# Splitting h into two fp16 parts in a serial recurrence on VectorE: a scan and a rounding constant, and the gates summed one after another

## The reference

```
def step(carry, xs):
    h, c = carry
    xi_t, xf_t, xg_t, xo_t = xs
    i_t = sigmoid(xi_t + h @ V_i)
    f_t = sigmoid(xf_t + h @ V_f)
    g_t = tanh(xg_t + h @ V_c)
    o_t = sigmoid(xo_t + h @ V_o)
    c_new = h * c + i_t * g_t
    h_new = o_t * tanh(c_new)
    return ((h_new, c_new), h_new)
(_, _), hs = lax.scan(step, (h0, c0), (xi, xf, xg, xo))
```

## Time and profile before

| | us |
|---|---|
| median of 3 runs | 3307.72 |
| lowest and highest | 3303.53, 3311.19 |
| span of the profiled execution | 3296.9 |
| VectorE busy | 1953.7 (59%) |
| TensorE busy, matmuls | 1510.9 (46%) |
| ScalarE busy | 1441.9 (44%) |
| GpSimd busy | 169.9 (5%) |

### The profile page before, as it was taken

How to read it: one execution, slowest core, us unless ns; L and a number is a source line. 1 busy time by engine, 2 the same in 40 slices (tenths; PEclk the granted TensorE clock), 3 DMA queues, 4 the chain that set the end, 5 groups by cost and what they waited for, 6 DMA issues and landing times.

```text
span 3296.9 us, 86333 instructions
## 1 busy us (share of the span) xinstructions
PE 1510.9 (46%) x26414; PEld 1141.6 (35%) x26414; DVE 1953.7 (59%) x13086; ACT 1441.9 (44%) x8446; POOL 169.9 (5%) x130
## 2 busy tenths in 40 slices
PE   4989575434343434333443434343434343434343
PEld 4444323333333333333333333333333333333333
DVE  5557896555555555555555555555555555555555
ACT  5331134444444444444444444444444444444444
POOL 0620271000000000000000000000000000000000
PEclk8999885555555555555555555555555555555555
DMA  6010000000000000000000000000000000000000
GB/s 225 1 32 0 0 5 1 2 3 2 3 2 3 2 3 2 3 2 3 2 2 3 2 3 2 3 2 3 2 3 2 3 2 3 2 2 2 3 2 15
DMA packets 13012, 29.04 MB, mean 9 GB/s; under 512 B 1971, under 2 KB 9654, under 8 KB 10422
## 3 DMA queue, kind: packets, MB, share of 16 engines
q1 hardware_dynamic: 10406, 22.02, 1.9%
q10 hardware_dynamic: 2064, 0.55, 0.1%
HBM read 21.52 MB, written 1.05 MB: 7 GB/s over the span
## 4 chain that ended last, share of the span: by engine, by line
ACT 37%; PE 37%; DVE 15%; issue 9%; DMA 1%; SPq 0%; DVEq 0%; POOL 0%; ACTq 0%; POOLq 0%
PE psum L490 21%; ACT work L663 18%; ACT work L659 11%; DVE work L984 11%; ACT work L655 8%; PE psum L412 4%; PE psum L494 3%; PE psum L353 2%; PE psum L474 2%; PE psum L473 2%; PE psum L364 1%; DVE work L898 1%; DVE FT L935 1%; DMA work<-in_adj_dram 1%; PE psum L392 0%
## 5 line engine op out<-in xcount | busy, mean ns | idle before, releaser
L490 PE MATMUL psum<-work,MASK 128*128 128x1 f16 x18432 | 951.5, 168 | 1656.3 <-DVE work L984 1582.5
L490 PEld LDWEIGHTS psum<-work,MASK 128*128 128x128 bf16 x18432 | 802.7, 107 | 1817.5 <-DVE work L984 1741.0
L655 ACT ACTIVATE work<-psum 128x1 f32<-128x1 f32 x2048 | 351.2, 172 | 1471.0 <-PE psum L494 1471.0
L979 DVE TENSOR_SCALAR work<-work 128x1 f32<-128x1 f32 x2048 | 314.6, 154 | 732.1 <-ACT work L659 732.1
L663 ACT ACTIVATE work<-psum,work 128x1 f32<-128x1 f32 x2048 | 720.2, 352 | 0.0
L494 PE MATMUL psum<-work,MASK 128*128 128x1 f16 x6144 | 575.5, 168 | 0.0
L984 DVE CUSTOM_DVE_ANT_0 work<-work 128x1 f16<-128x1 f32 x2048 | 331.5, 162 | 295.3
L494 PEld LDWEIGHTS psum<-work,MASK 128*128 128x128 f16 x6144 | 432.3, 107 | 0.0
L990 DVE SCALAR_TENSOR_TENSOR work<-psum,work 128x1 f32<-128x1 f32 x2048 | 430.7, 210 | 0.0
L659 ACT ACTIVATE work<-psum 128x1 f32<-128x1 f32 x2048 | 414.9, 203 | 20.8 <-PE psum L494 20.8
L987 DVE TENSOR_TENSOR work<-work 128x1 f16<-128x1 f32 x2048 | 332.3, 162 | 72.1
(11 more groups left out here) (132 smaller groups left out, 1005.2 us busy)
## 6 DMA issues: line engine op xcount, KB each, us to landing
work<-in_adj_dram SPq DMA_DIRECT2D x16, 1024.0 KB, 5.3
work<-in_L_ffn_Wd_dram SPq DMA_DIRECT2D x4, 512.0 KB, 6.0
out_dram<-work SPq DMA_DIRECT2D x4, 256.0 KB, 2.4
work<-in_L_ffn_bd_dram SPq DMA_DIRECT2D x1, 512.0 KB, 6.8
W<-in_L_ffn_W_dram ACTq DMA_DIRECT2D x1, 256.0 KB, 2.8
watt<-in_L_gnn_w_att_dram ACTq DMA_DIRECT2D x2, 64.0 KB, 7.2
work<-in_L_gnn_Wq_dram SPq DMA_DIRECT2D x1, 64.0 KB, 8.1
Wfc<-in_L_gnn_W_fc_dram ACTq DMA_DIRECT2D x1, 64.0 KB, 5.8
```

What stands on the lines that cost most here:

```text
L490: nc.tensor.matmul(bank(NGATE * k + gate)[:, col:col + 1], Vparts[:, gate, part, :], h1[:, q:q + 1], start=False, stop=False, skip_group_c ...
L655: nc.scalar.activation(sig_i[:, q], bank(NGATE * k)[:, col:col + 1], ACT.Sigmoid).then_inc(i_ready, 1)
L979: v.tensor_scalar(o_scaled[:, q], sig_o[:, q], SCALE_H, None, ALU.mult).then_inc(o_scaled_ready, 1)
```

## The change

h = (2^8 o) * tanh_c is split in another way. The constant ROUND_H = 1.5 * 2^20 is added to a number below 2^8 in fp32 and taken away again; what is left is the number rounded to a multiple of 1/8, which fp16 holds exactly.

- Line 979's instruction now writes two numbers, -2^8 o and 2^8 o, around a constant 0: `o_signs` times sig_o, sig_o being a scalar operand per partition.
- h1: a scan over three elements that starts from tanh_c. It multiplies by 2^8 o and adds 0, multiplies by 1 and adds ROUND_H, multiplies by 1 and adds -ROUND_H. Its third element, in fp16, is h1.
- h2: one instruction over three elements, (-2^8 o, 0, 2^8 o) * tanh_c + (-ROUND_H, ROUND_H, 0), whose sum over the elements goes out as h2 (accum_out, which adds a readout of the accumulator). It reads nothing that the scan wrote, and there is no wait between the two.
- The fp32 product into `ring_h` is an instruction of its own, and hc waits for it (h_ready).
- The waits ahead of the scan stand in the order o_scaled_ready, tanh_ready; those ahead of hc in the order h_ready, c_ready.
- TensorE: upper i (three), the wait for h2, lower i, upper g (three), lower g, upper o (three), lower o.
- Ten small constants are set ahead of the loop.

```
@@ tensor
                     pe.wait_ge(h1_ready, t + 1)
                     upper(0, 2, 1, 0)
-                    upper(1, 2, 1, 0)
-                    upper(2, 2)
                     pe.wait_ge(h2_part_ready, t + 1)
                     lower(0, i_summed)
+                    upper(1, 2, 1, 0)
                     lower(1, g_summed)
-                    upper(2, 1, 0)
+                    upper(2, 2, 1, 0)
                     lower(2, o_summed)
...
@@ vector
                     dve.wait_ge(o_ready, t + 1)
-                    v.tensor_scalar(o_scaled[:, q], sig_o[:, q], SCALE_H, None, ALU.mult).then_inc(o_scaled_ready, 1)
-
+                    v.tensor_scalar(o_signed[:, u % 2, 0:3:2], o_signs, sig_o[:, q], None, ALU.mult).then_inc(o_scaled_ready, 1)
+
+                    dve.wait_ge(o_scaled_ready, t + 1)
                     dve.wait_ge(tanh_ready, t + 1)
-                    dve.wait_ge(o_scaled_ready, t + 1)
-
-                    v.tensor_tensor_reduce(h1[:, r], tanh_c[:, q], o_scaled[:, q], 1.0, 0.0, ALU.mult, ALU.add,
-                                           ring_h[:, u:u + 1]).then_inc(h1_ready, 1)
-                    dve.wait_ge(h1_ready, t + 2)
-                    v.tensor_tensor(h2[:, r], ring_h[:, u:u + 1], h1[:, r], ALU.subtract).then_inc(h2_part_ready, 1)
+
+                    v.tensor_tensor_scan(h_steps[:, 1 - u % 2, 0:3], o_signed[:, u % 2, 2:5], round_up, tanh_c[:, q],
+                                         ALU.mult, ALU.add).then_inc(h1_ready, 1)
+
+                    v.scalar_tensor_tensor(h_sums, o_signed[:, u % 2, 0:3], tanh_c[:, q], round_back,
+                                           ALU.mult, ALU.add, accum_out=h2[:, r]).then_inc(h2_part_ready, 1)
+                    v.tensor_tensor(ring_h[:, u:u + 1], o_signed[:, u % 2, 2:3], tanh_c[:, q], ALU.mult).then_inc(h_ready, 1)
 
                     dve.wait_ge(hc_ready, t + 1)
                     v.scalar_tensor_tensor(c_[:, q], bank(6 + u % 2)[:, 0:1], sig_i[:, q], hc[:, q],
                                            ALU.mult, ALU.add).then_inc(c_ready, 1)
+                    dve.wait_ge(h_ready, t + 1)
                     dve.wait_ge(c_ready, t + 1)
                     v.scalar_tensor_tensor(hc[:, r], ring_h[:, u:u + 1], 1.0 / SCALE_H, c_[:, q],
                                            ALU.mult, ALU.mult).then_inc(hc_ready, 1)
```

More of the change, by code:

```diff
@@ L28 @@
 SCALE_H = 2.0 ** 8
+ROUND_H = 1.5 * 2.0 ** 20
 FP16_MAX = 65504.0
@@ L144, in build_program @@
         ring_h = region(N + HALF, STEPS)
-        c_, hc, tanh_c, sig_i, sig_o, o_scaled = (region(SMALL + 2 * k, 2) for k in range(6))
-        h1 = region(SMALL + 14, 1).bitcast(FP16)
+        c_, hc, tanh_c, sig_i, sig_o = (region(SMALL + 2 * k, 2) for k in range(5))
         h2 = region(SMALL + 16, 1).bitcast(FP16)
+        o_signed = region(SMALL + 18, 10, "p (q s) -> p q s", q=2)
+        h_steps = region(SMALL + 28, 4).bitcast(FP16).rearrange("p (q s) -> p q s", q=2)
+        h_sums = region(SMALL + 32, 3)
+        round_up = region(SMALL + 36, 3)
+        round_back = region(SMALL + 40, 3)
+        o_signs = region(SMALL + 44, 2)
         result = region(3 * N, N, "p (c t d) -> p c t d", c=NCH, t=TPC)
@@ L198, in build_program @@
         o_scaled_ready, h1_ready, h2_part_ready = sem("o_scaled_ready"), sem("h1_ready"), sem("h2_part_ready")
+        h_ready = sem("h_ready")
         c_ready, hc_ready, hh_ready = sem("c_ready"), sem("hc_ready"), sem("hh_ready")
@@ L489, in upper @@
                         for part in parts:
-                            nc.tensor.matmul(bank(NGATE * k + gate)[:, col:col + 1], Vparts[:, gate, part, :], h1[:, q:q + 1],
+                            nc.tensor.matmul(bank(NGATE * k + gate)[:, col:col + 1], Vparts[:, gate, part, :], h_steps[:, q, 2:3],
                                              start=False, stop=False, skip_group_check=True)
@@ L971, in _ @@
             v.memset(hc[:, 0:1], 0.0).then_inc(hc_ready, 1)
-            v.memset(h1[:, 0:1], 0.0).then_inc(h1_ready, 1)
+            for part, value in ((o_signs[:, 0:1], -SCALE_H), (o_signs[:, 1:2], SCALE_H),
+                                (o_signed[:, :, 1:2], 0.0), (o_signed[:, :, 3:5], 1.0),
+                                (round_up[:, 0:1], 0.0), (round_up[:, 1:2], ROUND_H), (round_up[:, 2:3], -ROUND_H),
+                                (round_back[:, 0:1], -ROUND_H), (round_back[:, 1:2], ROUND_H), (round_back[:, 2:3], 0.0)):
+                chain.step(v.memset(part, value))
+            v.memset(h_steps[:, 0, 2:3], 0.0).then_inc(h1_ready, 1)
             v.memset(h2[:, 0:1], 0.0).then_inc(h2_part_ready, 1)
```

## The result

| | before | after |
|---|---|---|
| median of 4 runs, us | 3305.72 | 3482.49 |
| lowest to highest, us | 3303.53 to 3311.19 | 3477.89 to 3483.36 |
| span of the profiled execution, us | 3296.9 | 3481.6 |

The ratio is 1.0532, 95% interval 1.0517 to 1.0547: the change makes the kernel slower by 177 us. 3538 was forecast, in a range of 3385 to 3650. The spans differ by more, 185 us: after's lies 1.8 under the time of its own run (3483.36), before's lies 6.6 under the lowest of its timed runs.

A forecast was written before the change was run, and what follows sets the result against it. The bound was taken to be the recurrence's 2048 serial steps, 1.35 us each. 0 + 0.04 + 0.07 = 0.11 us a step gives 225 us, plus 5 is +230: span 3527, time 3538 us, range 3385 to 3650.

The forecast's parts named there:

- The h split: Scan and h2 instruction on VectorE: independence buys back what scalar operands cost, 0 us a step (bounds -0.11, +0.08).
- The overlap of 0.08: VectorE: with no wait between, the h2 instruction starts 0.08 us before the scan ends.
- The gates in turn: TensorE's matmul order: lower g runs later, moving tanh of g and tanh of c by +0.04 us a step.
- The order of two waits: Ahead of the scan: tanh_c's wait, now second, is an instruction of its own, +0.07 us a step (bounds 0, 0.08).
- Side paths: hc and the o product beside the chain: both stay hidden, 0 us; hc's late end would cost 0.07.
- rival 1: hc ends last and holds tanh of c: +0.05 us more a step, 3640 us; chance 0.12.
- The small terms: Gate-input steps keep the same sum; longer VectorE program +4 us, ten constants +1 us: +5 us.
- the 10.8: Program start and end outside the profiled span: 10.8 us added to the forecast span of 3527 us.

The follow-up runs named there:

- a_dependent: Changed kernel with one wait added, so that the h2 instruction waits for the scan's h1_ready: 3746.79 us, ratio 1.1325.
- a_free_scan: As a_split_o, with ScalarE writing tanh_c into the scan's input, so the scan has four elements and no scalar operand: 3252.78 us, ratio 0.9825.
- a_oldgates: Changed kernel with the old order of matmuls (seven upper ones before the wait for h2): 3522.84 us, ratio 1.0645.
- a_split_o: Changed kernel with tanh_ready first ahead of the scan and the o product split into two products with constants: 3366.67 us, ratio 1.0177.
- a_waits: Changed kernel with the two waits ahead of the scan back in the old order, tanh_ready first: 3481.76 us, ratio 1.0521.
- b_turn: Kernel before with only the gates' matmuls reordered to sum i, g and o in turn: 3424.06 us, ratio 1.0348.
- b_noscale: Kernel before without line 979; line 984 multiplies by 2^8 itself and waits for tanh_ready, then o_ready: 3300.23 us, ratio 0.9970.
- b_noscale_turn: Kernel before without line 979, line 984 scaling itself, and with the gates summed in turn: 3352.58 us, ratio 1.0126.
- b_waits: Kernel before with only the two waits ahead of line 984 swapped, o_scaled_ready first, tanh_ready second: 3512.88 us, ratio 1.0615.

## Why the prediction was right, and where it was not

**The h split, 0: right.** h2's readout ends at the same time as line 987 did, to 0.01 us, for the reason given: an independence worth 0.13 (a_dependent) is spent on scalar operands. That the scan pays for its own was an inference from other instructions; a_free_scan shows it, at 0.06 us rather than 0.05. For the h2 instruction no run takes the scalar away; its 214 ns against the 159 of line 1007, of the same kind with a constant, stay a comparison. The overlap of 0.08 held too, to 0.01 (0.23 against a start at 0.14).

**The gates in turn, +0.04: a little too much.** Tanh of g moved by 0.04, but now that it doesn't follow close behind the i sigmoid it takes 0.156 us instead of 0.166 (line 657 against line 663 of the pages), so tanh of c moved by 0.03. The prediction called this what the reordering costs. That was right as a sum and wrong as a cause: a_oldgates has the new split with the old order, and there tanh of c starts 0.05 later than before the change (0.97 behind the scan for 0.92). So the split alone would cost that 0.05, by its later first matmul, and the new order takes 0.02 of it back.

**The order of two waits, +0.07: the price right, the order only half the cause.** 0.10 for 0.03 in the profile, and a_split_o takes it away. As a statement about the order alone it was wrong: a_waits shows that the o product came so late that the old order would have cost the same. That the term came out as forecast was in this part luck: the late o product, with its two elements and its scalar operand, would have brought it in either order. The forecast had that product 0.04 ahead of being needed; it ends at 2034.87 and the scan starts at 2034.97, so with a direct wait of 0.03 it was covered by 0.07, but only by the other wait's own price.

**Side paths.** hc ended at 0.83, at the early end of 0.82 to 0.94, 0.11 ahead of tanh of c, so rival 1 did not come. The 0.09 that was taken for ScalarE's second wait is shown by no run; at that price the cover would be nearly gone. The reading of the kernel before was wrong at one place: "line 979 ends at 1.15, 0.15 before it is needed" was no slack. A second wait stood in between, and b_turn, b_noscale and b_noscale_turn show that it held line 984 just as much as tanh of c did. The forecast for the change wasn't hurt, because the scan replaces line 984 and pays 0.07 where that pays 0.11.

**The small terms: wrong sign.** Steps behind gate inputs were said to shift as the others do. They did not: the timelines before and after have one such step each.

```profile
2001.72 0.16 DVE L984 CUSTOM_DVE_ANT_0 work<-work 128x1 f16<-128x1 f32 x1
...
2002.86 0.35 ACT L663 ACTIVATE work<-psum,work 128x1 f32<-128x1 f32 x1
...
2003.25 0.16 DVE L984 CUSTOM_DVE_ANT_0 work<-work 128x1 f16<-128x1 f32 x1
```

```profile
2010.76 0.23 DVE L995 TENSOR_TENSOR_SCAN work<-work 128x3 f16<-128x3 f32 x1
...
2011.83 0.35 ACT L669 ACTIVATE work<-psum,work 128x1 f32<-128x1 f32 x1
...
2012.28 0.23 DVE L995 TENSOR_TENSOR_SCAN work<-work 128x3 f16<-128x3 f32 x1
```

TensorE's own queue sets them: the next matmuls start when the gate inputs are through. In b_waits only the start of line 984 is late, by 0.11, and this step stays at 1.527 us, as the next matmuls wait that much less (0.33 behind line 984 for 0.44). In the changed kernel the gate inputs themselves begin 0.11 later behind the scan, so the matmuls start 0.45 behind it, about as before; but h1 and h2 are both there by then, in either kernel, and the new order lets tanh of c start 1.07 behind the scan where it was 1.14. That pays for the second wait's 0.07. And VectorE's longer program stalled less, not more: the wait on "issue" at the h2 instruction is 5.2 us where it was 15.8 at line 984.

```profile
DVE work L998 <- issue: 5.2, 32, 0.2
```

In sum: 0.098 a step for 0.11 (-24 us), gate steps (-10 us), and the small rest at -6 where +5 was forecast (-11 us): from the forecast 230 us to the 185 us of the spans. The other 10 us between 3538 and 3482 lie in the 10.8 that the forecast added to its span as start and end of the program. After's own run lies 1.8 above its span and the median of its runs 0.9; the 10.8 were for the most part a difference between executions of the kernel before.

## What to carry to other kernels

In a serial chain of small instructions the wait is priced like an instruction. Of several waits ahead of one instruction let the one that is satisfied last be written first, and count the others as late if they rise within their price of the start, 0.10 us ahead of the scan and 0.14 ahead of line 984's instruction; an apparent slack of that size in a timeline is none. Taking a dependence away wins (0.13 us here) only if the new form doesn't spend it elsewhere: look at each operand's kind, and feed a scan's per-partition scalar as an element where the producer can write it there. An order of matmuls is good or bad only together with the time at which their inputs come, so try it again after each change of that time.

## What the runs showed of the hardware

- On VectorE a second wait is an instruction of its own on the queue (0.02 us, DVEq L993 in the chain of after). Where it ends last, it costs 0.07 us ahead of the scan and 0.11 us ahead of line 984's instruction, above a direct wait's 0.03 (a_split_o, b_waits).
- With no wait between them the h2 instruction starts 0.09 us before the scan ends; with one it starts 0.12 later and the plain step is 0.13 longer (after, a_dependent).
- A scalar operand per partition costs the scan 0.06 us (226 against 167 ns for one element more).
- A scan over four fp32 elements takes 167 ns (a_free_scan), hardly more than a subtraction of one element with 162 (line 987 of before).
- ScalarE's sigmoid of o takes 0.20 us when it starts 0.05 after the start of the instruction ahead of it, and 0.17 when it starts 0.11 after it (before against after).
